# Three grouped attentions, from a loop of separate stages per group to one unrolled pipeline over all groups

## The chip, the cores and the metric

One core of one Trainium2 chip runs the whole program in one launch. The metric is the time of that launch on the device, in microseconds (us). TensorE (PE) multiplies, VectorE (DVE), ScalarE (ACT) and GpSimd (POOL) work on the results, SyncE (SP) issues the loads. Each engine runs its own instructions in their order in the program and waits only on semaphores.

## The reference

Four layers, each an attention and a feed-forward part, act on x (2 batches x 256 tokens x 512). Three attentions are dense and large; they are the ones that change:

```
x = x + attn0(norm(x), ctx)   # 32 heads of 128, 8 kv heads, rope, 512 keys
x = x + ffn0(norm(x))
x = x + attn1(norm(x), ctx)   # 16 heads of 96, 4 kv heads, keys = ctx + own (768)
x = x + ffn1(norm(x))
x = x + attn2(norm(x), ctx)   # 32 heads of 128, 4 kv heads, keys = ctx + own (768)
...
# one head: softmax(q @ k.T * scale + mask) @ v, then the heads' outputs @ wo
```

Two more layers' parts (ffn2, a small fourth attention, an 8-bit ffn3) follow.

## The kernel before

Every product is made from two planes of each operand, hi (rounded by ACT or POOL) and lo (what is left, by DVE or POOL), in three passes: hi by hi, lo by hi, hi by lo (`passes`, L299 to L301). The stages are called L0, L1 and L2 here. A stage runs over groups of four query heads: 8 groups in L0, 4 in L1, 8 in L2 (where two groups share one pair of key and value heads, `kv_every` 2). `Attention.loop` runs the groups in a hardware loop, the last one written out behind it.

Inside a group PE does, in this order: the four q projections, the k and v projections (each of 12 matmuls of 512 columns), then 16 score tiles in a pipeline of `PIPE` steps, and the four output projections `project(t)`. A score tile is 128 queries by 512 keys (L0) or 768 keys (L1, L2), and two tiles make one unit (one head and one batch). For tile i, step i holds `scores(i)`, `turn(i-2)` (the probabilities are transposed in pieces of four and two blocks, L563) and, at even i, `attend` of the unit whose tiles are i-4 and i-3 (L299 to L301 into `ps_o`).

DVE takes the largest score of each row (`nmax`, L754; in L0 one operation, L749, adds the mask, writes the tile to `l_p` and gives the largest), ACT takes the exponential (L681), DVE inverts its sum (L735), and the tile is scaled by ACT when even (L659), by DVE when odd (L759). After the transposes ACT makes the hi plane `l_pt_hi` (L669) and DVE the lo plane `l_pt_lo` (L777). In step i both engines do this for tile i-2, so that the planes of tile i-3 are done one step ahead of the `attend` that wants them. The transposes have three banks, `ps_t[p % 3]`.

L0 rotates its q and k: ACT swaps halves (L628, two operations), DVE multiplies with cos and sin (L707, L708), POOL adds (L477), ACT makes hi (L640) and DVE lo (L389, L387). The swap of the next tile is put ahead of the hi of this one. POOL also splits the loaded weights into their planes (L323, L325).

Of the kernel before, what the change touches and what calls it, by code (L numbers as in the profile page):

```python
# [20 lines left out]
ALU = mybir.AluOpType  # L21
# [7 lines left out]
P = 128  # L29
B, SQ, SK, D = 2, 256, 512, 512  # L30
T = B * SQ
# [35 lines left out]
def program(nc, A, out):  # L67
    ctx = ExitStack()
    with ctx:
# [44 lines left out]
        def attention_space(l):  # L114
# [9 lines left out]
            s.q = [take("q_hi", [P, HG, T], F32R), take("q_lo", [P, HG, T], F32R)]  # L124
# [3 lines left out]
            s.ot = [take("ot_hi", [P, HG, T], F32R), take("ot_lo", [P, HG, T], F32R)]  # L128
# [86 lines left out]
        ps_s = [ctx.enter_context(nc.psum_tensor(f"ps_s{i}", [P, 2, 512], F32)) for i in range(2)]  # L215
# [3 lines left out]
        ring = [ps_s[0][:, 0, :], ps_s[0][:, 1, :], ps_s[1][:, 0, :], ps_s[1][:, 1, :]]  # L219
# [30 lines left out]
        s_go = sem("tile_taken")  # L250
        s_rot = sem("rotation_parts")
        s_swap = sem("halves_swapped")
        s_nat = [sem("even_rows_in"), sem("odd_rows_in")]
# [3 lines left out]
        class Start:  # L257
# [3 lines left out]
            def __init__(self, g, hi, tile, piece, unit, q, kv, o, ra):  # L261
                self.g, self.hi, self.tile, self.piece, self.unit = g, hi, tile, piece, unit
                self.q, self.kv, self.o, self.ra = q, kv, o, ra
        counts = {n: 0 for n in ("g", "hi", "tile", "piece", "unit", "q", "kv", "o", "ra")}
# [8 lines left out]
        def attention_counts(l):  # L273
            n = l.groups
            kv = n // l.kv_every
            phase(l.name, g=kv * l.kv_tiles + n * 8, hi=kv * l.kv_hi + n * HG, tile=n * TILES,
                  piece=n * TILES * len(l.pieces), unit=n * UNITS, q=n, kv=kv, o=n,
                  ra=n * (HG + 2) if l.rope else 0)
# [121 lines left out]

        class Attention:
            def __init__(self, l, A, first_before, free=None):

                self.free = free
                self.l, self.s, self.c = l, SP[l.name], START[l.name]
                self.wkv, self.wq, self.wo = A[l.name + "_wkv"], A[l.name + "_wq"], A[l.name + "_wo"]
                self.first_before = first_before
                self.per = l.kv_every

            def loop(self, e, body):  # L410

                n = self.l.groups // self.per
                with e.Fori(0, n - 1) as i:
                    body(e, i, False)
                body(e, n - 1, True)

            def q_start(self, it, s):


                return it * (self.l.kv_tiles + 8 * self.per) + (self.c.g + (self.l.kv_tiles + 8 * s if s else 0))  # L420

            def o_start(self, it, s):
                return it * (self.l.kv_tiles + 8 * self.per) + (self.c.g + self.l.kv_tiles + 8 * s + HG)

            def hi_start(self, it, s):
                return it * (self.l.kv_hi + HG * self.per) + (self.c.hi + (self.l.kv_hi + HG * s if s else 0))

            def grp(self, it, s):
                return it * self.per + s
# [7 lines left out]
            def sp(self, e):  # L437
                l, c = self.l, self.c

                def body(e, it, last):  # L440
                    for s in range(self.per):
                        g = self.grp(it, s)
                        load(e, "o", None, self.wo[g], ("q", g + (c.q + 1)), parts=l.hd)
                        if s == self.per - 1 and not last:
                            load(e, "kv", None, self.wkv[it + 1], ("kv", it + (c.kv + 1)), cols=2 * l.hd)
                        if not (last and s == self.per - 1):
                            load(e, "q", None, self.wq[g + 1], ("o", g + (c.o + 1)), cols=HG * l.hd)
                self.loop(e, body)
# [12 lines left out]
            def pool(self, e):  # L461
                l, c, sp = self.l, self.c, self.s

                def body(e, it, last):
                    for s in range(self.per):
                        g = self.grp(it, s)
                        q0, o0 = self.q_start(it, s), self.o_start(it, s)
                        more = [("o", g + c.o, q0, p, l.hd, 512) for p in range(4)]
                        if s == self.per - 1 and not last:
                            more += [("kv", it + (c.kv + 1), o0, p, P, 2 * l.hd) for p in range(4)]  # L470
                        if not (last and s == self.per - 1):
                            more += [("q", g + (c.q + 1), o0, p, P, HG * l.hd) for p in range(4)]
                        if l.rope:
                            ra0 = it * (HG + 2) + c.ra
                            for t in range(HG + B):
                                e.wait_ge(s_rot, ra0 * 2 + (2 * t + 2))
                                e.tensor_tensor(sp.ra[:, t % 2, :], sp.ra[:, t % 2, :], sp.rb[:, t % 2, :], ALU.add)\  # L477
                                    .then_inc(s_ra, 1)
                        for job in more:
                            split(e, *job)  # L480
                self.loop(e, body)


            def pe(self, e):
# [3 lines left out]
                def body(e, it, last):  # L488
                    def bank(n, q0):

                        e.wait_ge(g_free, q0 + (n - 3))
                        return ring[n % 4]
                    for s in range(self.per):
                        g = self.grp(it, s)
                        q0, o0 = self.q_start(it, s), self.o_start(it, s)

                        def project_in(o, role, c0, src, lo, first=False):

                            for d in range(DK):
                                if first:  # L500
                                    e.wait_ge(g_free, c.g - 3 + d)
                                    e.wait_ge(w_rdy["q"], g * 8 + (8 * c.q + 2 * d + 2))
                                mm = passes(e, o[0:hd, :], planes(W[role], slice(None), d, slice(c0, c0 + hd)),
                                            planes(src, slice(None), d, slice(lo, lo + 512)), d == 0, d == DK - 1)
                            mm.then_inc(g_full, 1)
                        for hh in range(HG if s == 0 else HG - 1):
                            project_in(bank(hh, q0), "q", hh * hd, xT, 0, hh == 0)
                        if s == 0:

                            e.wait_ge(w_rdy["kv"], it * 8 + (8 * c.kv + 8))  # L510
                            e.wait_ge(s_csplit, DK)
                            for n, (src, lo) in enumerate([(cT, b * SK) for b in range(B)] + ([(xT, 0)] if l.self_keys else []), HG):
                                project_in(bank(n, q0), "kv", 0, src, lo)
# [1327 lines left out]
```

## Time and profile before

| | us |
|---|---|
| median of 3 runs | 2329.51 (2327.69 to 2330.35) |
| span of the profiled execution | 2328.4 |
| stage L0, first q projection to last output projection | 593.8 |
| stage L1 | 357.3 |
| stage L2 | 643.8 |
| one group of L0 after the first | 72.3 |
| one unit (two tiles) in the middle of an L2 group | 5.65 |

The stages' borders are the starts of their first projection matmul (18.7, 683.1 and 1084.3 us) and the ends of their last ones. The rest of the span, 733.5 us, is norms, feed-forward parts and the fourth attention. PE's busy time counts the modelled length of a matmul, which overlaps its neighbours' and can hide a short wait; the distance of two starts is the better measure of what one costs.

### The profile page before, as it was taken

Reading aid. Unit: us, or ns where it says so; the run is one execution under the profiler, and the core shown is the slowest. Engines: PE = TensorE matmul, PEld = TensorE weight load, DVE = VectorE, ACT = ScalarE, POOL = GpSimd, SP = SyncE. Lnnn points to the kernel's source line nnn. Section 1 sums busy time; section 2 is a strip of 40 time slices with the busy share of each in tenths; the row PEclk is TensorE's granted clock in tenths of the full one; section 3 lists DMA queues with packets and bytes.
Section 4 is the critical chain, followed back from the end, with each engine's and each line's share of the span. In section 5 each row is a group of like instructions: output and inputs, shape, how many; then the busy total and the mean of one; then the engine's idle time right before and its main releaser. Section 6 shows DMA issues by size and latency. Waiting matters only on the chain. (4 is left out here: it accounts for less than half of the span.)

```text
span 2328.4 us, 34351 instructions
## 1 busy us (share of the span) xinstructions
PE 2063.1 (89%) x11612; PEld 1707.9 (73%) x11616; DVE 1558.6 (67%) x3108; ACT 1142.4 (49%) x2338; POOL 901.6 (39%) x850
## 2 busy tenths in 40 slices
PE   5989999899879999987999999999988899996667
PEld 4777777777658788786888888888876677775535
DVE  5677666776657466475764674576564695897999
ACT  3556455565316256351653563555540594782430
POOL 7355533554432322224141233222316674662612
PEclk9999999999989999998999999999999999998889
DMA  3111001110110001001010011001101101002301
GB/s 137 46 45 45 18 27 45 45 36 18 62 30 25 14 22 34 19 12 62 28 37 20 28 37 32 33 19 39 37 28 43 37 1 55 1 19 77 127 18 37
DMA packets 20011, 87.16 MB, mean 37 GB/s; under 512 B 2736, under 2 KB 8624, under 8 KB 11440
## 3 DMA queue, kind: packets, MB, share of 16 engines
q1 hardware_dynamic: 19888, 85.55, 10.6%
q8 instruction: 74, 1.21, 0.2%
q14 instruction: 49, 0.40, 0.1%
HBM read 84.49 MB, written 1.05 MB: 37 GB/s over the span
## 5 line engine op out<-in xcount | busy, mean ns | idle before, releaser
L777 DVE TENSOR_TENSOR l_pt_lo<-ps_t,l_pt_hi 128x512 fp32r<-128x512 f32 (+1 forms) x512 | 283.2, 584 | 87.3 <-ACT l_pt_hi L669 80.1
L323 POOL TENSOR_TENSOR wo_hi<-raw_big,one 128x512 fp32r<-128x512 f32 (+2 forms) x116 | 123.0, 1060 | 489.6 <-PE ps_s L301 460.0
L669 ACT ACTIVATE l_pt_hi<-ps_t 128x512 fp32r<-128x512 f32 (+1 forms) x512 | 243.8, 515 | 108.1 <-PE ps_t L563 103.8
L563 PE MATMUL ps_t<-ident,l_p 128*128 128x128 f32 x1664 | 244.8, 277 | 45.9 <-DVE l_pt_lo L777 29.4
L563 PEld LDWEIGHTS ps_t<-ident,l_p 128*128 128x128 f32 x1664 | 191.9, 141 | 84.3 <-DVE l_pt_lo L777 37.7
L299 PE MATMUL ps_o<-l_pt_hi,l_v_hi 128*128 128x256 f32 (+1 forms) x704 | 211.7, 301 | 14.3 <-DVE l_pt_lo L777 14.3
L323 POOL TENSOR_TENSOR wq_hi<-raw_big,one 128x512 fp32r<-128x512 f32 (+1 forms) x120 | 126.1, 1051 | 199.7 <-PE ps_o L529 98.2
L299 PE MATMUL ps_s<-l_k_hi,l_q_hi 128*128 128x512 f32 (+3 forms) x512 | 195.9, 383 | 7.7 <-DVE l_k_lo L387 3.9
L754 DVE TENSOR_REDUCE nmax<-ps_s 128x1 f32<-128x768 f32 x192 | 183.0, 953 | 28.6 <-PE ps_s L301 28.3
L301 PE MATMUL ps_o<-l_pt_hi,l_v_lo 128*128 128x256 f32 (+1 forms) x704 | 200.0, 284 | 0.0
L300 PE MATMUL ps_o<-l_pt_lo,l_v_hi 128*128 128x256 f32 (+1 forms) x704 | 199.9, 284 | 0.0
L681 ACT ACTIVATE l_p<-ps_s,nmax 128x768 f32<-128x768 f32 x192 | 173.6, 904 | 28.2 <-DVE nmax L754 28.2
L477 POOL TENSOR_TENSOR l_ra<-l_ra,l_rb 128x512 f32<-128x512 f32 x48 | 76.3, 1591 | 271.8 <-DVE l_rb L708 270.7
L300 PE MATMUL ps_s<-l_k_lo,l_q_hi 128*128 128x512 f32 (+3 forms) x512 | 180.8, 353 | 0.0
L301 PE MATMUL ps_s<-l_k_hi,l_q_lo 128*128 128x512 f32 (+3 forms) x512 | 180.6, 353 | 0.0
L1125 POOL TENSOR_TENSOR l_p<-l_p,rinv 128x512 f32<-128x512 f32 x128 | 132.3, 1040 | 84.1 <-DVE rinv L1295 84.1
L299 PE MATMUL ps_s<-xT_hi,wq_hi 128*128 128x512 f32 (+1 forms) x384 | 152.6, 397 | 10.5 <-issue 10.0
L325 POOL TENSOR_TENSOR wq_lo<-raw_big,wq_hi 128x512 fp32r<-128x512 f32 (+1 forms) x120 | 156.4, 1303 | 9.4
L325 POOL TENSOR_TENSOR wo_lo<-raw_big,wo_hi 128x512 fp32r<-128x512 f32 (+2 forms) x116 | 152.0, 1310 | 9.1
L659 ACT ACTIVATE l_p<-l_p,rinv 128x768 f32<-128x768 f32 (+1 forms) x160 | 135.9, 849 | 34.9 <-DVE rinv L735 34.5
L299 PEld LDWEIGHTS ps_o<-l_pt_hi,l_v_hi 128*128 128x128 f32 (+1 forms) x704 | 130.2, 185 | 29.4 <-DVE l_pt_lo L777 21.2
L300 PE MATMUL ps_s<-xT_lo,wq_hi 128*128 128x512 f32 (+1 forms) x384 | 151.1, 394 | 0.0
(309 smaller groups left out, 5552.1 us busy)
## 6 DMA issues: line engine op xcount, KB each, us to landing
raw_big<-in_l_wq SPq DMA_DIRECT2D x18, 1024.0 KB, 5.0
raw_big<-in_l_wo SPq DMA_DIRECT2D x18, 1024.0 KB, 4.9
raw_big<-in_f_w SPq DMA_DIRECT2D x10, 1024.0 KB, 5.0
raw_kv<-in_l_wkv SPq DMA_DIRECT2D x12, 512.0 KB, 5.7
q_nat<-in_f_w1n SPq DMA_DIRECT2D x4, 1024.0 KB, 4.8
q_nat<-in_f_w2n SPq DMA_DIRECT2D x4, 1024.0 KB, 4.8
raw_big<-in_l_wq SPq DMA_DIRECT2D x4, 768.0 KB, 4.7
raw_big<-in_l_wo SPq DMA_DIRECT2D x4, 768.0 KB, 5.5
```

What stands on the lines that cost most here:

```text
L299: pe.matmul(o, a[0], b[0], start=start, stop=False)
L300: pe.matmul(o, a[0], b[1], start=False, stop=False)
L301: return pe.matmul(o, a[1], b[0], start=False, stop=stop)
L323: pool.tensor_tensor(hi, w, one[0:parts, 0:1].to_broadcast([parts, cols]), ALU.mult).then_inc(w_rdy[role], 1)
L325: pool.tensor_tensor(lo, w, hi.bitcast(F32), ALU.subtract).then_inc(w_rdy[role], 1)
L563: mm = e.transpose(ps_t[p % 3][:, k * P:(k + 1) * P], sp.p[:, i % 3, (k0 + k) * P:(k0 + k + 1) * P], ident[:, :])
L659: e.activation(pr, pr, ACT.Copy, scale=rinv[:, i - 1:i]).then_inc(s_scl[0], 1)
L669: e.activation(sp.pt[u % 2][0][:, k0:k0 + nk, qt * P:(qt + 1) * P], ps_t[p % 3][:, 0:nk * P].rearrange("p (k q) -> p k q", q=P), ACT.Copy) ...
L681: e.activation(sp.p[:, i % 3, :], src, ACT.Exp, bias=nmax[:, i:i + 1], scale=-1.0 if l.rope else 1.0, accum_out=rsum[:, i:i + 1]).then_inc ...
L754: e.tensor_reduce(nmax[:, i:i + 1], ps_flat(i)[:, 0:l.keys], AX.X, ALU.max, negate=True).then_inc(s_max, 1)
L777: e.tensor_tensor(pt[1], ps_t[p % 3][:, 0:nk * P].rearrange("p (k q) -> p k q", q=P), pt[0].bitcast(F32), ALU.subtract).then_inc(s_tlo, 1)
L1125: e.tensor_tensor(l3p[:, i % 4, :], l3p[:, i % 4, :], rinv[:, i % TILES:i % TILES + 1].to_broadcast([P, SK]), ALU.mult).then_inc(s3["scl"], 1)
```

## The change

The loops go. `Attention.place` writes one list of slots for all groups of a stage, one slot for each score tile (128 in L0, 64 in L1, 128 in L2), with a few before the first and four behind the last. The projections become jobs; each is cut into four parts of three matmuls, and the parts are dealt out over the slots of a neighbouring group: three parts a slot in L0 and L2, four in L1. In group g's slots run the output projections of group g-1, the q projections of group g+1, the key and value projections of batch 1 for this group and of batch 0 for the next. The jobs take turns on two banks, `ring[3]` and `ps_t[2]`, so the transposes have two banks in place of three. The own keys' projection of L1 and L2 (one of 512 columns) becomes two of 256.

The order within slot k is, with the engines' waits in brackets:

```
PE   scores(k) [largest or exp of k-2; the own keys' part also exp of k-1]
     job parts [job's bank]; values turned [bank]; turn(k-2) [bank: lo of the piece two before]
     even k: attend of tiles k-4, k-3 [lo of k-3]
ACT  hi of tile k-3; hi of the unit's output; L0: hi of the job ended in k-1 [POOL's add]
     exp(k); hi of values; job ended in k: swap or hi; even k: scale
DVE  largest(k) [scores(k)]; lo of tile k-3; lo of output; L0: lo of the job ended in k-1
     1/sum [exp(k)]; lo of values [their hi]; job ended in k: rotate [swap], lo, or add to x
     odd k: scale
POOL L0: add of the job ended in k; then pieces of weights
```

The core of the diff (of the two loops over the slots the first is PE's, the second DVE's):

```diff
-            s.q = [take("q_hi", [P, HG, T], F32R), take("q_lo", [P, HG, T], F32R)]
+            s.q = [[take(f"q{i}_{n}", [P, HG, T], F32R) for n in ("hi", "lo")] for i in range(2)]
-            s.ot = [take("ot_hi", [P, HG, T], F32R), take("ot_lo", [P, HG, T], F32R)]
-        ps_s = [ctx.enter_context(nc.psum_tensor(f"ps_s{i}", [P, 2, 512], F32)) for i in range(2)]
+        ps_s = ctx.enter_context(nc.psum_tensor("ps_s", [P, 4, 512], F32))
+        ORDER = {
+            "l0": ["k1 o0 o1 v1 o2 o3 q0 k0 q1 v0 q2 q3"],
+            "l1": ["k1 K1 o0 v1 V1 o1 o2 o3 q0 k0 K0 q1 v0 V0 q2 q3"],
+            "l2": ["k1 K1 o0 v1 V1 o1 o2 o3 q0 q1 q2 q3", "o0 o1 o2 o3 q0 q1 k0 K0 q2 v0 V0 q3"],
+        }
+        FIRST = {"l0": "q0 q1 q2 q3 k0 v0", "l1": "q0 k0 K0 q1 v0 V0 q2 q3", "l2": "q0 k0 K0 q1 v0 V0 q2 q3"}
...
+                            job(name, own, [g * TILES + (4 * n + part) // per for part in range(4)])
...
+            def bank(self, j):
+                return (ring[3], ps_t[2][:, :])[j.n % 2]
...
+                def take_turn_bank(p):
+                    if p >= 2:
+                        e.wait_ge(s_tlo, c.piece + p - 1)
+                    return ps_t[p % 2]
...
+                for k in self.slots:
+                    if 0 <= k < self.N:
+                        scores(k)
+                    for j, part in self.parts.get(k, ()):
+                        project(j, part)
+                    for j in self.values.get(k, ()):
+                        turn_values(j)
+                    if 0 <= k - 2 < self.N:
+                        turn(k - 2)
+                    if self.unit_at(k) is not None:
+                        attend(self.unit_at(k))
...
+                for k in self.slots:
+                    if 0 <= k < self.N:
+                        largest(k)
+                    if 0 <= k - 3 < self.N:
+                        turned_lo(k - 3)
...
+                    for j in self.ended.get(k - 1, ()):
+                        if j.rope is not None:
+                            operand_lo(j, sp.ra[:, j.rope % 2, :], s_qk)
...
+                    for j in self.values.get(k, ()):
+                        e.wait_ge(s_thi, c.piece + self.v_piece[j.n] + 1)
...
+                    for j in self.ended.get(k, ()):
+                        if j.rope is not None:
+                            rotate(j)
```

The outputs of a group are written over its own q planes, and q has two sets of planes. In the job names a capital letter is an own-key job of 256 columns. The fourth attention uses the same banks under other names.

## Rows read from the trace of the kernel before

**Rows 1.** The page: the span.
```profile
span 2328.4 us, 34351 instructions
```

**Rows 2.** The stretches view: start:end, length, busy of PE, PEld, DVE, ACT, POOL, clock, DMA.
```profile
18.70:612.50 593.80, 538.53 (x2882) 439.80 (x2881) 393.55 (x853) 329.95 (x678) 282.75 (x245) 0.98 0.10 35
683.10:1040.40 357.30, 343.97 (x2066) 288.60 (x2064) 208.69 (x400) 176.38 (x362) 87.01 (x96) 0.99 0.08 23
1084.30:1728.10 643.80, 619.85 (x3794) 546.51 (x3792) 396.20 (x745) 338.83 (x698) 167.53 (x160) 1.00 0.09 30
104.00:176.30 72.30, 66.45 (x361) 54.39 (x360) 48.14 (x106) 40.67 (x84) 33.98 (x30) 1.00 0.10 36
...
176.33:187.21 10.88, 10.88 (x50) 9.01 (x48) 5.15 (x9) 4.82 (x8) 2.96 (x2) 1.00 0.00 0
...
227.36:231.61 4.25, 3.96 (x29) 3.38 (x28) 3.75 (x11) 3.58 (x9) 0.00 (x0) 1.00 0.18 75
1460.02:1465.67 5.65, 5.65 (x44) 5.34 (x43) 4.99 (x12) 4.77 (x10) 0.00 (x0) 1.00 0.01 3
```

**Rows 3.** The timeline of PE in an L2 unit: start, length, then the instruction.
```profile
1460.02 0.40 PE L299 MATMUL ps_s<-l_k_hi,l_q_hi 128*128 128x512 f32 x1
...
1461.07 0.82 PE L563 MATMUL ps_t<-ident,l_p 128*128 128x128 f32 x6
1461.64 0.47 PE L299 MATMUL ps_s<-l_k_hi,l_q_hi 128*128 128x512 f32 x1
...
1462.77 0.82 PE L563 MATMUL ps_t<-ident,l_p 128*128 128x128 f32 x6
1463.41 0.38 PE L299 MATMUL ps_o<-l_pt_hi,l_v_hi 128*128 128x256 f32 x1
```

**Rows 4.** The waits of PE in stage L0: us in total, times, longest.
```profile
PE ps_o L299 <- DVE l_pt_lo L777: 14.3, 29, 0.8
PE ps_t L563 <- DVE l_v_lo L387: 9.7, 8, 1.3
```

**Rows 5.** The waits of PE in stage L2.
```profile
PE ps_t L563 <- DVE l_pt_lo L777: 20.0, 23, 1.7
```

**Rows 6.** The timeline of PE where one L0 group ends and the next begins.
```profile
176.10 0.39 PE L301 MATMUL ps_s<-wo_hi,l_ot_lo 128*128 128x512 f32 x1
176.33 0.39 PE L299 MATMUL ps_s<-xT_hi,wq_hi 128*128 128x512 f32 x1
```

**Rows 7.** The timeline of DVE in the same L2 unit.
```profile
1461.27 0.96 DVE L754 TENSOR_REDUCE nmax<-ps_s 128x1 f32<-128x768 f32 x1 [0.21 <-PE ps_s L301]
1462.34 1.02 DVE L777 TENSOR_TENSOR l_pt_lo<-ps_t,l_pt_hi 128x512 fp32r<-128x512 f32 x2
```

**Rows 8.** The timeline of DVE in an L0 unit.
```profile
228.44 0.69 DVE L749 CUSTOM_DVE_ANT_0 l_p<-ps_s,l_mask 128x512 f32<-128x512 f32 x1
...
229.32 0.69 DVE L777 TENSOR_TENSOR l_pt_lo<-ps_t,l_pt_hi 128x512 fp32r<-128x512 f32 x1 [0.18 <-ACT l_pt_hi L669]
```

**Rows 9.** The timeline of all engines in the start of stage L0.
```profile
36.45 2.48 POOL L477 TENSOR_TENSOR l_ra<-l_ra,l_rb 128x512 f32<-128x512 f32 x2
...
37.74 0.63 ACT L640 ACTIVATE l_q_hi<-l_ra 128x512 fp32r<-128x512 f32 x1 [11.86 <-POOL l_ra L477]
38.40 1.21 ACT L628 ACTIVATE l_rb<-ps_s 64x512 f32<-64x512 f32 x2
...
40.25 0.68 DVE L708 TENSOR_TENSOR l_rb<-l_rb,l_sin 128x512 f32<-128x512 f32 x1
...
41.01 1.66 POOL L477 TENSOR_TENSOR l_ra<-l_ra,l_rb 128x512 f32<-128x512 f32 x1 [2.07 <-DVE l_rb L708]
...
52.59 0.50 PE L299 MATMUL ps_s<-l_k_hi,l_q_hi 128*128 128x512 f32 x1 [0.48 <-DVE l_k_lo L387]
```

**Rows 10.** The timeline of ACT in the same L2 unit.
```profile
1462.46 0.91 ACT L681 ACTIVATE l_p<-ps_s,nmax 128x768 f32<-128x768 f32 x1
1463.25 0.21 ACT L681 ACTIVATION_READ_ACCUMULATOR l_p<-ps_s,nmax 128x1 f32 x1
```

More of the change, by code:

```diff
@@ L438, in sp @@
                 l, c = self.l, self.c
[L440 to L448, printed above, removed]
+                for g in range(l.groups):
+                    before = self.raw_before(g)
+                    if g + 1 < l.groups:
+                        load(e, "q", None, self.wq[g + 1], before, cols=HG * l.hd)
+                        before = ("q", c.q + g + 2)
+                    kv = g // l.kv_every
+                    if g % l.kv_every == 0 and kv + 1 < self.kvs:
+                        load(e, "kv", None, self.wkv[kv + 1], ("kv", c.kv + kv + 1), cols=2 * l.hd)
+                    load(e, "o", None, self.wo[g], before, parts=l.hd)
             def pool_first(self, e):
@@ L462, in pool @@
                 l, c, sp = self.l, self.c, self.s
[L464 to L480, printed above, removed]
@@ new lines, in own_o @@
+                def own_o(g, piece):
+                    used = self.full(self.find["o", g - 1, 3, False]) if g else c.g
+                    split(e, "o", c.o + g, used, piece, parts=l.hd)
+                if not l.rope:
+                    for g in range(l.groups):
+                        for piece in range(4):
+                            next_q(g, piece)
+                        for piece in range(4):
+                            next_kv(g, piece)
+                        for piece in range(4):
+                            own_o(g, piece)
+                    return
@@ new lines, in project_out @@
+                def project_out(j):
+                    e.wait_ge(g_full, self.full(j))
+                    if j.kind == "v":
+                        if j.stage >= 4:
+                            old = [v for v in self.jobs if v.stage == j.stage - 4][0]
+                            e.wait_ge(s_T, c.piece + self.v_piece[old.n] + 1)
+                        e.tensor_copy(xn[0:hd, j.stage % 4, 0:j.width], self.bank(j)[0:hd, 0:j.width]).then_inc(g_free, 1)
+                        return
+                    t = j.i
+                    if j.g:
+                        e.wait_ge(g_free, self.full(self.find["o", j.g - 1, t, False]))
+                    e.tensor_tensor(x[:, t, :], self.bank(j), x[:, t, :], ALU.add).then_inc(g_free, 1)
+                    if j.g == l.groups - 1 and t < TT - 1:
+                        e.wait_ge(g_free, self.full(j))
+                        e.bn_stats(st[:, t, :], x[:, t, :])
```

631 lines of the change are left out of this document (317 added, 314 removed).

## The prediction

> **What bounds the kernel now.** I read the stretches view first. The three attention stages fill 593.8 + 357.3 + 643.8 = 1594.9 us of the 2328.4 us span [rows 1, 2]; the other 733.5 us are code that the change leaves alone. In them PE is busy 91%, 96% and 96%, while DVE has 66%, 58% and 62% and ACT and POOL less: PE sets the pace, and what a rewrite can win is only the time in which PE waits. Next I priced PE's work by distances between starts. Four q projections, 48 matmuls, take 10.88 us [rows 2]: one job 2.72, one part of three matmuls 0.68. An L2 unit takes 5.65, of which about 0.07 is a wait (the second turn lasts 1462.77 to 1463.41, 0.64, the first 0.57) [rows 2, 3]: 5.58. For an L0 unit I scale the pieces of that one (12 products 1.5, six score matmuls 1.44, two turns 0.76): 3.7 of the 4.25 measured [rows 2].
>
> Work per group is then: L0 8 x 3.7 + 12 x 2.72 + 0.8 (values turned) = 63.0; L1 8 x 5.58 + 14 x 2.72 + 1 = 83.7; two groups of L2 16 x 5.58 + 22 x 2.72 + 1 = 150.1. Stages: 504, 335 and 600, 1439 together. PE stands still for the rest: 90, 22 and 44 us, 156 in all. That is the most the change could win. The waits views name the owners: in L0 products that wait for DVE's lo planes (14.3) and transposes behind the values (9.7) [rows 4], in L2 transposes that wait for lo planes, 20.0 [rows 5]. A unit inside a group waits little; most of the loss lies where a group fills and drains.
>
> **What the change removes.** Filling and draining happen once a stage. The branch at the end of a group is removed too, and by the rows it costs nothing: the first matmul of a new group starts 0.23 us after the last of the old, the normal distance [rows 6]. The Trainium skill ("Runtime: NRT & Kernel Launch", Instruction fetch mechanics) says that a taken branch outside the window forces a fetch, so that unrolling helps; by that rule the 13 branches would each give something back, by the row they give 0. I put in 0.
>
> The number of matmuls stays, but for the own-key jobs (24 of 512 columns become 48 of 256): +0.5 us a stage. The loads are the same in number and size. SP issues the next q's before this group's o's; POOL is busy 34 of 72.3 us in an L0 group [rows 2], and each weight is split at least two slots ahead of its first use, so I cost that order at nothing.
>
> **What it adds: a chain inside each slot of L1 and L2.** With two turn banks and two pieces a tile, the first piece of turn(k-2) needs the lo of tile k-3's first piece. DVE makes that in slot k, behind largest(k), which waits for this slot's scores. From the rows: DVE starts its largest 1.25 after the scores began [rows 3, 7], takes 0.96, then the lo 0.69 [rows 7, 8]: 2.90 after the slot's start, about 2.85 since neighbours on DVE overlap a little. PE's scores end at 1.05 (1460.02 to 1461.07) or, behind a turn, 1.13 (1461.64 to 1462.77) [rows 3]. With three full parts PE gets to the turn at 3.1: hidden, by 0.2. With m parts it waits 1.8 - 0.68 m. The same chain stood one step earlier before, since both engines did tile i-2 in step i. So a slot without jobs costs nearly what a full one does, and the work that lies in the prologue (8 jobs) and the tail (4 jobs) is missing in the slots without making them shorter. L1: 12 empty slots x 1.8 = 21.6. L2: in the first group 0.4 + 1.8 + 0.4 + 5.4 + 1.1, in the last 1.1 + 10 x 1.8: 28.3. Jobs of half width leave gaps too: 7 x 0.4 = 2.8 in L1, 2.6 for each of four key and value pairs in L2, 10.
>
> **Values in the turn ring.** A slot that turns values puts their piece between two of the probabilities', so the second piece of turn(k-2) needs DVE's lo of the values. The values are turned at about 3.3, plus 0.2 to ACT, 0.63 hi, 0.69 lo [rows 8, 9]: 4.8 against 3.7 for PE, and the gap before them besides; 1.6 lost for a full job, 0.7 for the half one behind it. Seven such pairs in each of L1 and L2: 16 each.
>
> **L0's rope chain.** One piece a tile frees the turn bank a slot earlier, but ACT now makes hi of the last rotated job before exp(k), and exp(k) stands before the next swap; before, the swap went ahead. Rotations in neighbouring slots follow each other by: POOL's add 1.24 (two in 2.48) to 1.66, taken 1.5; hi 0.63; exp 0.83 (the 768-wide one is 0.91 [rows 10]); swap 1.21; two multiplications 1.3; handovers 0.1: 5.5 [rows 9]. A slot of PE is 3.1 (odd) or 4.65 (even). Jobs end in slots 9, 10, 11. The first is rotated 5.0 after slot 9 began, the third 11.0 later, the scale adds 0.6: 16.6, where PE's three slots take 10.9. DVE comes 5.7 late to slot 12, then does largest and lo (1.4) [rows 8], and attend, which PE would reach at 3.2, starts 3.9 late. The pair in 14 and 15, held up by the values' lo in 14, costs 2.7, the one in 17 0.7: 7.4 for each of seven groups, 52, and 1 in the last. The old loss was 9.3 (72.3 - 63.0). Empty pairs of slots take 6.2 here (DVE's chain through exp and scale), not 3.7: six of them, 15. In the start the adds begin at 36.45 as before [rows 9]; then each rotation waits for hi of the one before: 4.75 each. The first scores come at 58.0, not 52.6 [rows 9]: 39.3 us for six jobs of 2.72, so 23 of wait.
>
> **Changes of operand.** Scores behind a turn cost 0.08 more than behind products [rows 3]; inside projections there is nothing. New seams, one or two a slot: between 0 and 0.08, taken 0.05, x 320 slots = 16 (6, 3, 6). Tails 3, 2, 3; L2's start at the lower clock 3, as now.
>
> **The sum.** L0: 504 + 23 + 53 + 15 + 3 + 6 = 604, against 593.8: +10. L1: 335 + 0.5 + 21.6 + 2.8 + 16 + 2 + 3 = 381, against 357.3: +24. L2: 600 + 0.5 + 28.3 + 10 + 16 + 3 + 3 + 6 = 667, against 643.8: +23. Together +57 on the profiled 2328.4: 2385; the median of the runs is 1.1 higher, so 2387.
>
> **Rivals.**
> *DVE late in full slots too.* The cover there is 0.2 us, and odd slots end with an operand's lo and the scale. If DVE starts 0.4 later than that cover in each of the 96 even slots of L1 and L2, that is +38: 2425. For it: POOL's splits run beside DVE's operations. Against it: in the steady unit of L2 DVE is busy 4.99 of 5.65 and still on time [rows 2], and the new full pair is 9.7 long.
> *The rope chain stays hidden.* If PE never sees it (it would, once the period is over 3.9), L0 loses 53 less: 2334. Against it: the 5.5 is a sum of measured pieces.
> *A full pipeline.* The other sign: the lo chain is not what ends PE's wait in a slot, so that PE runs at its work. It decides from there: if lo of tile k-3 is done by the end of the scores, as it is now, a slot costs its matmuls. Then 1439 + start 23 + tails 8 + seams 16 = 1486, 109 less than now: 2220. For it: DVE and ACT have a third of their time free. Against it: the order of DVE's slot puts largest first, and that can't start before the scores.
>
> **How the numbers follow.** A difference under 0.2% (4.7 us) can't be told from none here. Forecast 0.65; late DVE 0.15; hidden rope 0.12; full pipeline 0.08. The bounds of single terms: seams 0 to 26 for 16, rope 45 to 60, the values' 32 down to 20, empty slots 45 to 70: 2350 to 2410 for the forecast alone. With most of the late-DVE case and without hidden rope and full pipeline, the range is 2345 to 2430. Faster: 0.08 and a little of the rope case, 0.10; same: the rest of the rope case, 0.08; slower 0.82.
>
> **What would show it.** In the last group of L2 two neighbouring slots should take about 9.2 us with no job in them (5.65 now), PE waiting for `l_pt_lo` before the first transposes. Full pairs should take 9.7 to 9.8. The slot with values should show a wait of more than 1 us in the middle of a turn, for `l_v_lo`. In L0 the products of slot 12 should start some 3 us late behind lo planes, with DVE idle for the swap before. The first scores of L0 should come near 58. I am wrong if empty slots are shorter than 4 us on average, or if PE's waits for lo planes shrink in L2.

## The result, and the profile after

The changed kernel takes 2410.7 us (median; 2409.4 to 2415.7) beside 2329.4 us before: a ratio of 1.0353, 95% interval 1.0339 to 1.0368. The forecast was 2387 in a range of 2345 to 2430. The sign and the mechanism were right; 22 us of waits and of lower clock were missing from the sum, which named 57 us where the profiled executions show 79 (2407.6 against 2328.4); on the medians it is 24 us short.

The page's span, and the stretches view of the three stages, which answers to [rows 1, 2] (from the first q projection to the last matmul of the last output projection):

```profile
span 2407.6 us, 32169 instructions
...
19.88:631.85 611.97, 544.94 (x2880) 460.11 (x2880) 379.67 (x850) 335.35 (x676) 272.05 (x244) 0.94 0.10 34
701.39:1084.22 382.83, 350.80 (x2162) 296.03 (x2160) 208.40 (x403) 179.96 (x370) 87.84 (x96) 0.98 0.07 21
1130.61:1808.68 678.07, 623.64 (x3890) 545.01 (x3888) 387.80 (x755) 344.90 (x706) 169.83 (x160) 0.99 0.08 29
```

Before, the same stages ran 18.74 to 612.74, 683.13 to 1038.18 and 1084.28 to 1727.65. The end of L1 in [rows 2], 1040.40, and with it the 357.3 of the table of the time before, is 2.2 too late: the stage before was 355.1 us long, and the sum's +24 for L1 is +26 against that. So L0 ends 19.1 later (1.1 of it at its start), L1 is 27.8 longer, L2 34.7, and the stretches between and behind them are 2.4 shorter: 79.2. TensorE's share fell from 91, 97 and 96% to 89, 92 and 92%.

The stretches view of single slots and groups says where. In order: one L0 group; a pair of L2 slots without a job; a full pair; the L2 slot in which values are turned; slot 12 of the L0 group, and the products at its end; slot 8 of L2's first group:

```profile
122.09:194.03 71.94, 67.23 (x364) 57.39 (x362) 47.58 (x106) 41.45 (x85) 32.87 (x30) 0.95 0.11 37
...
1749.24:1758.67 9.43, 5.95 (x44) 5.33 (x43) 4.96 (x10) 4.93 (x10) 6.93 (x13) 1.00 0.28 112
1250.46:1260.14 9.68, 9.68 (x63) 8.58 (x62) 5.32 (x12) 4.94 (x10) 1.54 (x2) 1.00 0.00 1
...
1298.50:1305.94 7.44, 6.22 (x46) 5.39 (x45) 4.18 (x8) 4.10 (x8) 0.00 (x0) 1.00 0.01 2
...
173.52:182.39 8.87, 6.15 (x31) 5.37 (x29) 5.39 (x12) 5.67 (x11) 4.78 (x5) 0.84 0.00 1
179.69:182.39 2.70, 2.70 (x12) 2.70 (x13) 0.92 (x2) 2.39 (x5) 2.62 (x3) 0.50 0.00 0
...
1186.92:1196.08 9.16, 7.42 (x32) 6.86 (x31) 2.89 (x5) 3.07 (x6) 5.26 (x5) 0.50 0.30 102
```

A pair without any projection costs 9.43 us, a pair with six parts in it (one and a half jobs, 18 matmuls) 9.68: the slot is as long as a chain, not as long as its matmuls. The waits view of PE in the stage L0, then in L2, answers to [rows 4, 5]:

```profile
PE ps_o L298 <- DVE l_pt_lo L801: 41.4, 20, 2.8
PE ps_t L298 <- DVE l_ra L826: 11.5, 2, 10.9
...
PE ps_t L687 <- DVE l_pt_lo L801: 34.8, 38, 1.8
PE ps_t L687 <- DVE l_v_lo L863: 10.1, 14, 1.0
PE ps_t L694 <- DVE l_pt_lo L801: 4.0, 8, 1.6
PE ps_s L298 <- DVE l_q_lo L853: 3.7, 4, 0.9
```

In L0 the products' wait for lo planes went from 14.3 to 41.4 us, in L2 that of the transposes from 20.0 to 34.8. (The 10.9 for `l_ra` stands in the start of L0, at 40.5 us, where a key projection waits for a bank that a rotation has to free.) How an empty slot of L2 runs, in the timeline of PE and then of DVE (the bracket holds the idle time before the instruction and its releaser); compare [rows 3, 7]:

```profile
1758.67 0.40 PE L298 MATMUL ps_s<-l_k_hi,l_q_hi 128*128 128x512 f32 x1
...
1759.61 0.28 PE L300 MATMUL ps_s<-l_k_hi,l_q_lo 128*128 128x256 f32 x1
1761.62 0.85 PE L687 MATMUL ps_t<-ident,l_p 128*128 128x128 f32 x6 [1.74 <-DVE l_pt_lo L801]
1762.23 0.48 PE L298 MATMUL ps_s<-l_k_hi,l_q_hi 128*128 128x512 f32 x1
```
```profile
1759.92 0.96 DVE L793 TENSOR_REDUCE nmax<-ps_s 128x1 f32<-128x768 f32 x1 [3.60 <-PE ps_s L300]
1760.80 1.01 DVE L801 TENSOR_TENSOR l_pt_lo<-ps_t,l_pt_hi 128x512 fp32r<-128x512 f32 x2
```

DVE sits idle for 3.60 us until this slot's scores are done, takes their largest, and only then the lo planes of a tile that ScalarE had ready long before; PE has nothing left to do and waits 1.74 us for them. The sum had 1.8.

### The profile page after: what moved, and what is told of

It is laid out like the page before. It is cut to its first block and busy times, and to the rows that moved or that the text cites. A ratio compares the mean times of both kernels' runs of the same rounds, so it can differ in the third digit from the quotient of the medians.

```text
span 2407.6 us, 32169 instructions
## 1 busy us (share of the span) xinstructions
PE 2074.9 (86%) x11804; PEld 1730.7 (72%) x11808; DVE 1546.4 (64%) x3132; ACT 1158.5 (48%) x2354; POOL 894.6 (37%) x850
## 5 line engine op out<-in xcount | busy, mean ns | idle before, releaser
L687 PE MATMUL ps_t<-ident,l_p 128*128 128x128 f32 x1664 | 245.0, 277 | 79.6 <-DVE l_pt_lo L801 59.9
L298 PE MATMUL ps_o<-l_pt_hi,l_v_hi 128*128 128x256 f32 (+1 forms) x832 | 254.7, 306 | 42.3 <-DVE l_pt_lo L801 41.4
L300 PE MATMUL ps_o<-l_pt_hi,l_v_lo 128*128 128x256 f32 (+1 forms) x832 | 242.1, 291 | 0.0
L299 PE MATMUL ps_o<-l_pt_lo,l_v_hi 128*128 128x256 f32 (+1 forms) x832 | 241.8, 291 | 0.0
L298 PEld LDWEIGHTS ps_o<-l_pt_hi,l_v_hi 128*128 128x128 f32 (+1 forms) x832 | 159.2, 191 | 49.5 <-DVE l_pt_lo L801 49.2
L589 POOL TENSOR_TENSOR l_ra<-l_ra,l_rb 128x512 f32<-128x512 f32 x48 | 66.5, 1385 | 254.7 <-DVE l_ra L826 254.7
L300 PEld LDWEIGHTS ps_o<-l_pt_hi,l_v_lo 128*128 128x128 f32 (+1 forms) x832 | 160.7, 193 | 0.0
L299 PEld LDWEIGHTS ps_o<-l_pt_lo,l_v_hi 128*128 128x128 f32 (+1 forms) x832 | 160.4, 193 | 0.1
```

What stands on the lines that cost most here:

```text
L298: pe.matmul(o, a[0], b[0], start=start, stop=False)
L299: pe.matmul(o, a[0], b[1], start=False, stop=False)
L300: return pe.matmul(o, a[1], b[0], start=False, stop=stop)
L687: mm = e.transpose(o[:, kk * P:(kk + 1) * P], sp.p[:, k % 3, at:at + P], ident[:, :])
```

## The experiments

All times are medians of runs, against 2328 to 2330 for the kernel before in the same session. Stage lengths are from the stretches view, in us (L1 and L2 as above; L0 from its first q projection):

| kernel | L0 | L1 | L2 | time | ratio to before |
|---|---|---|---|---|---|
| before | 594.0 | 355.1 | 643.4 | 2329.4 | |
| changed | 612.0 | 382.8 | 678.1 | 2410.7 | 1.0353 |
| 1 lower parts first | 605.8 | 373.9 | 669.9 | 2388.9 | 1.0254 [1.0236, 1.0271] |
| 5 scaling deferred | 591.9 | 366.7 | 643.0 | 2340.6 | 1.0042 [1.0025, 1.0059] |
| 6 values early | 584.4 | 355.4 | 629.4 | 2305.8 | 0.9900 [0.9882, 0.9918] |
| 7 upper part late | 581.1 | 355.5 | 629.5 | 2303.0 | 0.9893 [0.9875, 0.9910] |
| 10 swap early | 551.6 | 355.8 | 629.6 | 2274.5 | 0.9763 [0.9750, 0.9776] |

**1. Lower parts first.** VectorE takes the lo of tile k-3 before the largest of tile k:

```diff
                 for k in self.slots:
-                    if 0 <= k < self.N:
-                        largest(k)
                     if 0 <= k - 3 < self.N:
                         turned_lo(k - 3)
+                    if 0 <= k < self.N:
+                        largest(k)
```

> Only DVE's order in a slot changes: the lo planes of tile k-3 come ahead of largest(k), in all three stages. Theory 1 (the lo chain behind the scores): a pair of empty slots in L2, 9.43 us now, falls to about 7.8 (the scale of the odd tile then holds the next lo), full pairs stay at 9.69, the slots with values lose at most 0.3; L1 falls by about 15 us, L2 by about 20, L0 by about 19 because every product after a cluster of rotations starts 0.7 earlier; in all about 2358. Rival (PE is held by job banks or by late weights, not by the lo planes): empty pairs stay at 9.4 and the time within 5 us of 2411. Rival (PE's own work and seams are the bound): no change either.

Measured: 2388.9, 22 us less than the changed kernel. The chain was real, since its order alone moved every stage, but the gain was smaller than expected: an empty pair of L2 still took 9.1 us on average (7.64, 1.63, 6.19, 2.36, 7.85, 1.62 for six neighbouring slots of the last group). The timeline of DVE there, and one row of ACT's, show the next holder; the last row is PE's in a slot with values:

```profile
1732.51 0.94 DVE L793 TENSOR_REDUCE nmax<-ps_s 128x1 f32<-128x768 f32 x1
1734.51 0.17 DVE L860 RECIPROCAL rinv<-rsum 128x1 f32<-128x1 f32 x1 [1.06 <-ACT l_p L753]
1736.16 1.02 DVE L801 TENSOR_TENSOR l_pt_lo<-ps_t,l_pt_hi 128x512 fp32r<-128x512 f32 x2 [1.49 <-ACT l_pt_hi L735]
...
1734.71 0.94 ACT L775 ACTIVATE l_p<-l_p,rinv 128x768 f32<-128x768 f32 x1 [0.23 <-DVE rinv L860]
...
1282.36 0.44 PE L687 MATMUL ps_t<-ident,l_p 128*128 128x128 f32 x2 [2.08 <-DVE l_v_lo L863]
```

Largest, exp, reciprocal and scale of one tile stand in one slot, each on the other engine than the one before; the hi and then the lo of an older tile are queued behind them. The slots with values got longer too: the seven of L2 took 8.1 to 9.6 in place of 7.44, some 12 us in all where 0.3 a slot had been allowed for. The largest now came later, with it the exp, and behind the exp the hi and lo of the values: PE waited 2.08 for them in the slot of the row, where it had waited 0.97, and 19.8 us in all of L2 in place of 10.1.

**2. The swap first.** In L0 the swapped copy is made before the hi of the job before it, and the rotation before its lo:

```diff
-  ACT: hi of job ended in k-1; exp(k); ...; swap of job ended in k; scale
+  ACT: exp(k); ...; swap of job ended in k; hi of job ended in k-1; scale
-  DVE: lo of job ended in k-1; 1/sum(k); ...; rotate; scale
+  DVE: 1/sum(k); ...; rotate; lo of job ended in k-1; scale
```

> Only L0 changes: ACT swaps the job ended in slot k ahead of the hi of the job before it, and DVE rotates ahead of that job's lo, as in the kernel before. Theory 2 (the chain add, hi, exp, swap, rotate sets L0's stalls): the first scores come about 4.5 us earlier, near 52.5; the distance of two rotations in neighbouring slots falls only from 5.5 to about 5.1, since largest, exp, swap, rotate, lo and scale still follow one another, so L0 falls by 10 to 15 us in all. Rival (POOL's add is the whole stall): the slots after 9, 10 and 11 lose their 4 us, L0 falls by 30 or more. L1 and L2 stay within 1 us.

Measured: 2414.4 in a single run. The first scores came 5.4 us earlier (51.60 against 57.04) and L0 ended 4.6 earlier, its inner groups as long as before (71.8 in the mean, both times). The gain in the start is shown; in the groups the order of these two changed nothing. That the whole is not shorter lies in parts that the edit doesn't touch: L1 was 4.7 longer, since one of its first slots fell to the lower clock and took 9.16 in place of 6.74, and the one two behind it 8.21 in place of 6.65; the stretches outside the three stages were 5 longer; L2 was the same. A difference of 4 us in one run is not worth reading further.

**3. The rotation a slot later**, on top of experiment 1: a job that ends in slot k is rotated at the head of slot k+1 and split in k+2; k0 is projected second.

```diff
+  DVE: lo(k-3); rotate job ended in k-1; largest(k); lo of job ended in k-2; ...
+        FIRST = {"l0": "q0 k0 q1 q2 q3 v0", ...
```

> On top of lo first: in L0 a job ended in slot k is swapped in slot k, rotated by DVE in slot k+1 ahead of largest, and split in slot k+2; the first key job moves up to second place in the prologue so that the first scores don't wait for its lo. Theory 2: the rope chain no longer stands inside one slot, its stalls of 7 us a group shrink to about 1, the first scores come near 51; L0 falls by about 50 us below that of lo first, the whole to about 2310. Rival (L0 is held by DVE's total work or by the job banks): L0 stays within 10 us of that of lo first.

Measured: 2417.0, ratio 1.0376 [1.0359, 1.0394]. Wrong by 107 us, with the sign wrong. The first scores came at 51.24, but each inner group of L0 took 75.1 us. The waits view of PE in L0, a row of its timeline, and the stretch behind that row:

```profile
PE ps_s L298 <- DVE l_ra L828: 38.7, 21, 3.8
...
207.84 0.50 PE L298 MATMUL ps_s<-wo_hi,l_q_hi 128*128 128x512 f32 x1 [3.75 <-DVE l_ra L828]
...
209.00:212.00 3.00, 3.00 (x17) 2.90 (x15) 1.46 (x3) 1.68 (x5) 2.92 (x4) 0.53 0.00 0
```

The rotation also frees the job's bank, and there are only two of them: moved by a slot, it holds up the projections. (The place of k0 was changed in the same run; it bears on the first scores, not on the inner groups.) What I had weighed was only who waits for the rotated operand.

**4. L2 without most of its q projections**, in the changed kernel. This kernel leaves out 11 of the 12 matmuls of each q projection of L2's groups 2 to 7 (264 matmuls, at 0.227 each 59.9 us of TensorE's work), so its output differs.

```diff
+                        if l is L2 and j.g >= 2:
+                            if part == 3:
+                                e.matmul(o[0:hd, :], W["q"][0][:, part, ...], xT[0][:, part, 0:T], ...).then_inc(g_full, 1)
+                            return
```

> Leaves out part of the computation: in L2 the q projections of groups 2 to 7 do one matmul of twelve, so 264 matmuls of 512 columns are gone, 59.9 us of PE's work at 0.227 each; jobs, banks and waits stay. Theory 1: the slots that held these parts become empty slots, which cost nearly as much as full ones (9.43 against 9.69 a pair), so L2 falls by only 4 to 8 us. Rival (PE's work is the bound in full slots and the chain has slack): L2 falls by 40 to 60 us.

Measured: 2407.3 in a single run, 3.4 us less for 59.9 us of work, and not even these in L2: that stage took 677.9 where it had 678.1, and L0, which the edit doesn't touch, was 2.4 shorter. Emptied pairs of slots took 5.87 + 3.56 = 9.43, and PE's waits for lo planes in L2 took over what the work had filled (34.8 us, 38 times, in the changed kernel):

```profile
PE ps_t L692 <- DVE l_pt_lo L806: 78.0, 66, 2.3
```

What the emptied pairs gave, 0.25 each, was lost again, in part in slot 12 of the third and fifth groups, which took 7.9 in place of 6.1 with a wait of 2.3 in it. So in the changed kernel this work of TensorE in L2 has no price of its own. This is the run that decides for the chain.

**5. Scaling deferred**, on top of 1: reciprocal and scale of tile k-1 stand in slot k.

```diff
   DVE: 
+       1/sum(k-1)
        lo(k-3); lo of the output; largest(k)
+       scale(k-1) if odd
-       1/sum(k) ... scale(k) if odd
   ACT: hi(k-3); hi of the output; hi of rotated job
+       scale(k-1) if even
        exp(k)
-       ... scale(k) if even
```

> The pipeline as changed, with the lower parts of the turned tile ahead of the largest on VectorE (as in the first experiment), and with the reciprocal of the row sums and the scaling of tile k-1 moved from the end of slot k-1 into slot k, so that no engine waits inside a slot for scores, largest, exp, reciprocal and scale in a row. Theory 1 (slots are as long as the in-order chain of their engines, and the first experiment only gave the chain another holder, the largest, exp, reciprocal and scale of an odd tile): an empty pair of L2 falls from 9.2 to between 5.7 and 7 us, L1 to about 360 us, L2 to about 645, the full pairs of L2 stay at 9.69; in all 2330 to 2350. Rival (TensorE is held by its clock or by turn banks whatever the order): empty pairs stay at 9 us, in all 2385 or more.

Measured: 2340.6, 48 us less than 1. An empty pair of L2 now takes 5.80 + 1.62 = 7.42 (expected 5.7 to 7, a little short of the truth), a full one still 9.68, the stage 643.0 as expected; L1 took 366.7 where 360 had been expected. Of the 27 us that L2 lost against 1, about 12 lie in the seven slots with values, which take 7.3 again (8.5 in the first group).

**6. Values early**, on top of 5: they are turned behind the scores, and their hi and lo are not kept behind exp and the projections' end.

```diff
   PE:  scores(k)
+       turn_values
        project parts
-       turn_values
   ACT: 
+       hi of values
        exp(k)
-       hi of values
   DVE: largest(k)
+       lo of values
        scale(k-1) if odd; ...
-       lo of values
```

> The kernel of the run with deferred scaling, and the values of a slot are turned on TensorE right after the scores, their upper part taken on ScalarE ahead of the exp and their lower part on VectorE right behind the largest. Theory 1: the slots with values in them (4 a group in L1, 2 a group of keys in L2) lose the wait of TensorE for the lower part of the values, about 1.8 us each, so some 14 us in L1 and 14 in L2 and little in L0: in all 20 to 30 us less than the run before it. Rival (the wait passes to the turn bank of the tile behind it): less than 8 us.

Measured: 2305.8, 35 us less than 5, and 1.0% less than the kernel before. L1 lost 11.3, L2 13.5, L0 7.5; the pair with the values in it went from 7.32 + 4.64 to 6.18 + 3.93 in L2. More than expected by L0's part, for which I had put in little.

**7. The upper part late**, on top of 6: in L0 ScalarE takes the hi of the rotated operand behind exp(k) in place of ahead of it, so that exp doesn't wait for GpSimd's addition.

```diff
-  ACT: hi of job ended in k-1; ...; exp(k); swap
+  ACT: ...; exp(k); hi of job ended in k-1; swap
```

> The kernel of the run with early values, and the upper part of a rotated operand of L0 is taken on ScalarE behind the exp in place of ahead of it, so that the exp of a slot doesn't wait for GpSimd's addition. L1 and L2 have no such step and stay as they are. Theory 1 (the long slots of L0, 7.5 to 8.9 us against 4.7 in the others, come from the rotation's chain ending ahead of the exp): slots 0 and 12 of each group fall to 5 to 6 us, L0 20 to 30 us shorter than in the run before it. Rival (the chain is only late elsewhere: its lower part then ends the slot, or scores wait for the operand): L0 changes by less than 5 us.

Measured: 2303.0; L0 3.3 us shorter. The rival was right: slot 12 went from 7.6 to 7.1, slot 14 from 5.2 to 5.9. Even the 3.3 are no gain of the new order inside the groups: in kernel 6 four of the six inner groups took 68.1 and two, with a longer slot 12, took 69.6 and 70.9; in kernel 7 all six took 68.4 to 68.5. The timeline of DVE in front of slot 12's products, then of PE, shows the waits that were left:

```profile
306.75 0.69 DVE L809 TENSOR_TENSOR l_k_lo<-l_ra,l_k_hi 128x512 fp32r<-128x512 f32 x1 [1.41 <-ACT l_k_hi L762]
307.99 0.69 DVE L825 TENSOR_TENSOR l_rb<-l_rb,l_sin 128x512 f32<-128x512 f32 x1 [0.54 <-ACT l_rb L771]
...
310.04 0.35 PE L298 MATMUL ps_o<-l_pt_hi,l_v_hi 128*128 128x256 f32 x1 [2.15 <-DVE l_pt_lo L802]
```

**8. Experiment 4's omission again, in kernel 7** (the same 264 matmuls left out, the diff is that of 4).

> The kernel of the run with the late upper part, in which the q projections of L2's groups 2 to 7 do one of their twelve matmuls: the same 264 matmuls, 59.9 us of TensorE's work, that were left out of the changed kernel for a gain of 3.4 us. Theory 1 (after the reordering TensorE itself sets the length of L2's full slots, 9.69 us a pair, and the chain of a slot without projections is 5.8 us a pair): nearly the whole of the work comes back as time, between 45 and 60 us less, about 2250. Rival (the slots are still bound by a chain of the other engines): less than 15 us.

Measured: 2280.0, 23 us less where the changed kernel gave 3.4 (L2 by itself 26 less, where the changed kernel gave 0.2). Between the two theories. In the full slots of kernel 7 TensorE is busy 75.67 of 76.00 us (the stretch 1200 to 1276 of its trace, the first row below), so there it is the bound; once the work is out, the next chains are met soon: an emptied pair took between 7.0 and 9.7 (5.10 + 1.86 in the second group, 7.78 + 1.87 in the fifth), and slot 8 of the second group, behind an emptied one, 7.19 in place of 6.02. In the stretch 1150 to 1600 PE waited 9.6 us for ScalarE's exp and 9.3 for lo planes (second and third row), where in kernel 7 it had waited 1.0 in all. Of the 59.9 us TensorE bound 23; the rest was already covered by chains just below it.

```profile
1200.00:1276.00 76.00, 75.67 (x502) 68.28 (x501) 50.54 (x101) 43.14 (x91) 14.86 (x16) 1.00 0.08 32
...
PE ps_s L298 <- ACT l_p L761: 9.6, 15, 0.9
PE ps_t L692 <- DVE l_pt_lo L807: 9.3, 12, 1.3
```

**9. The key second**, on top of 7.

```diff
-        FIRST = {"l0": "q0 q1 q2 q3 k0 v0", ...
+        FIRST = {"l0": "q0 k0 q1 q2 q3 v0", ...
```

> The kernel of the run with the late upper part, with one order changed: the six first projections of L0 run as q0, k0, q1, q2, q3, v0 in place of q0 to q3, k0, v0. The first scores need q0 and k0, and waited 4.4 us for k0's lower part. Theory 1 (the chain of k0's rotation holds the first scores): first scores 3 to 4.4 us earlier and 2299 in all. Rival (the first six projections wait for one another's banks whatever their order, or k0's weights come later than q's): no change, 2303.

Measured: 2306.4, ratio 0.9905 [0.9891, 0.9918]: no difference from 7 that can be told. The first scores came 1.8 earlier (55.36), and the first group of L0 took 66.2 in place of 61.1, 3.0 of it in its slot 0. Here earlier first scores were worth nothing, since the first slots were longer by more.

**10. The swap early**, on top of 7: swap and rotation of the job that ends in slot k stand ahead of exp(k).

```diff
   ACT: hi of values
+       swap of job ended in k
        exp(k); hi of job ended in k-1
-       swap of job ended in k
   DVE: largest(k); lo of values; scale(k-1) if odd
+       rotate job ended in k          [also waits until ra's last reader is done]
        lo of job ended in k-1
-       rotate job ended in k
```

> The kernel of the run with the late upper part (2303), and in L0 the swapped copy of a projection that ends in slot k is made on ScalarE ahead of the exp of slot k, with VectorE's rotation right behind the largest and the lower part of the operand before it after that; L1 and L2 stay as they are. In the slots with a rotation VectorE there waited 1.0 to 1.4 us for the upper part and 0.54 for the swap, and a chain of three such slots ended with TensorE waiting 2.1 us for the turned tile (slot 12 of each L0 group, 7.1 us against 4.7). Theory 1 (these two waits inside the slot make the period of a rotation 5.5 us): slot 12 falls to 5 us and slots 0 and 2 to 4.7, L0 15 to 30 us shorter, in all 2273 to 2288. Rival (ScalarE, with swap, exp and upper parts in a row, takes VectorE's place, or GpSimd's addition is what is late): less than 5 us either way.

Measured: 2274.5, 28 us less than 7 and 2.4% less than before. L0 is 29.5 shorter than in 7. Inner L0 groups take 65.1 us (72.3 before, 71.9 after the change, 68.4 in 7), slot 12 5.4, slot 2 4.7, slot 0 5.4 where 4.7 had been expected; about 10 of the 29.5 lie in the start and the first group (first scores 51.4 against 57.2, the group 56.8 against 61.1). The stretches view of its stages, and the waits of PE in L0 from 105 to 540:

```profile
19.89:571.45 551.56, 521.80 (x2880) 440.63 (x2880) 389.36 (x850) 329.33 (x676) 283.16 (x244) 0.99 0.11 38
643.86:999.65 355.79, 343.42 (x2162) 292.89 (x2160) 208.42 (x404) 177.75 (x370) 87.72 (x96) 0.99 0.08 23
1046.17:1675.78 629.61, 613.84 (x3890) 544.42 (x3888) 392.55 (x756) 341.17 (x706) 169.79 (x160) 1.00 0.08 31
...
PE ps_o L298 <- DVE l_pt_lo L803: 7.7, 15, 1.7
```

**11. The splits after the scale**, in the changed kernel: GpSimd begins the next q weights of L1 and L2 after VectorE's last scale of the group.

```diff
                     for g in range(l.groups):
+                        if g:
+                            e.wait_ge(s_scl[1], (c.tile + TILES * g) // 2)
```

> The changed kernel with one wait more: in L1 and L2 GpSimd begins the splits of a group's next q weights after VectorE has scaled the last tile of the group before. In the changed kernel this scale (TENSOR_SCALAR, 768 columns) took 1.70 us where it stood beside GpSimd's splits and 0.61 elsewhere, and TensorE then waited 0.78 us for the turned tile in slot 0 of L2's odd groups (7.0 us against 6.0). Theory 1 (the two engines get in each other's way, and this is what the four slots lose): the scale takes 0.61 in those four places, slot 0 of the odd groups 6.0, L2 4 us shorter, in all 2407. Rival (slot 0 is long because four q projections ended before it, whatever GpSimd does): the slots stay at 7.0 and the total at 2411.

Measured: 2412.4, ratio 1.0361 [1.0342, 1.0380], and L2 675.7 against 678.1. Below, DVE's scale and GpSimd's split in the changed kernel and PE's wait behind them; then the same scale in this one.

```profile
1229.72 1.70 DVE L876 TENSOR_SCALAR l_p<-l_p,rinv 128x768 f32<-128x768 f32 x1
...
1229.72 1.29 POOL L324 TENSOR_TENSOR wq_lo<-raw_big,wq_hi 128x512 fp32r<-128x512 f32 x1
...
1233.03 0.85 PE L687 MATMUL ps_t<-ident,l_p 128*128 128x128 f32 x6 [0.78 <-DVE l_pt_lo L801]
```
```profile
1232.46 0.61 DVE L878 TENSOR_SCALAR l_p<-l_p,rinv 128x768 f32<-128x768 f32 x1
```

The mechanism is shown: the scale takes 0.61, slot 0 of the second, fourth and sixth groups 6.03, 6.00 and 6.01 in place of 7.0. They are three, not four: the last group has no next weights, and its slot 0 took 6.03 in the changed kernel too. L2 is 2.4 shorter, three times 1.0 less three times 0.2 in slot 2. In the total this can't be seen: L0, which the edit doesn't touch, was 614.7 in this profile against 612.0.

## Why the prediction was right in sign and 22 us short

**PE sets the pace, and only its waits can be won.** Right for the kernel before. For the changed one it holds no longer: experiment 4 took 59.9 us of PE's work out of L2 and left its length as it was.

**The chain in each slot of L1 and L2.** Right, and the decisive step. Forecast: 1.8 of wait in an empty slot, 9.2 a pair, full pairs 9.7 to 9.8; measured 1.74, 9.43 and 9.68. The pair is 0.23 over the forecast because PE's own work in it is 5.95 and not the 5.58 that I took from a unit nearly without a wait; the two waits are 0.12 shorter. L1 came to 382.8 where the sum had 381. No run gave the transposes their third bank back, so what two banks cost by themselves, beside the order of the engines, stays open.

**Values in the turn ring.** Right: PE's wait for `l_v_lo` in the middle of a turn, 0.97 and then 0.50 (I had 1.6 and 0.7 with the gap before), the slot 7.44 in place of 6.0 and the one behind it 4.64 in place of 3.7. The claim of "more than 1 us" for one wait was a little high. Experiment 6 is its test. PE's two waits, in the slot with values and in the one behind it:

```profile
1303.51 0.44 PE L687 MATMUL ps_t<-ident,l_p 128*128 128x128 f32 x2 [0.97 <-DVE l_v_lo L863]
...
1310.37 0.44 PE L687 MATMUL ps_t<-ident,l_p 128*128 128x128 f32 x2 [0.50 <-DVE l_v_lo L863]
```

**Full slots are covered.** Right for most and wrong in two places of each odd group of L2, and this was the first term that is missing, 8 us. In slot 0 of three of them the cover of 0.2 was gone, by GpSimd: 1.0 each (experiment 11). The rival "DVE late in full slots" had the right reason in three slots and not in 96. In slot 3 of all four PE waited 0.94 for the lo of the last unit's output, which o2's last part reads (`ps_s <- l_q_lo`, 3.7 in all): 4.90 against 3.69, 1.2 each. The sum had no term for where the o projections stand, and it took for granted that POOL's splits cost DVE nothing in a full slot.

**L2's start.** The sum had 3 us for the lower clock, as before. Slot 8 of the first group is an empty slot at a granted clock of 0.50 and took 9.16, not 5.87: 3.3 more. PE had been busy 1.95 of the 3.92 us before it. With the 8 of the odd groups this comes to the 11 us by which L2 passed its 667.

**L0's rope chain.** The mechanism is shown by experiment 10; 2 and 7 alone did little for the groups. The products of slot 12 started 2.72 late (the sum had 3.9, the claim "some 3"); slots 0 and 1 took 11.5 and slots 12 and 13 took 12.2, where a full pair is 7.8, and slots 6, 10 and 14 some 0.4 more than their neighbours: 71.9 a group, where the forecast came to 71.1 (63.0 of work, 7.4 and the seams). The lateness was 1.2 smaller than in the sum, and as much was paid in a way that the sum didn't know: in six of the seven groups TensorE came out of the wait at the lower clock, and the twelve products took up to 2.70 in place of 1.5 (the row 179.69 to 182.39). In front of them stood DVE's wait for the swap, as forecast:

```profile
176.69 0.69 DVE L824 TENSOR_TENSOR l_rb<-l_rb,l_sin 128x512 f32<-128x512 f32 x1 [1.07 <-ACT l_rb L766]
...
178.91 0.69 DVE L801 TENSOR_TENSOR l_pt_lo<-ps_t,l_pt_hi 128x512 fp32r<-128x512 f32 x1
...
179.69 0.55 PE L298 MATMUL ps_o<-l_pt_hi,l_v_hi 128*128 128x256 f32 x1 [2.72 <-DVE l_pt_lo L801]
```

L0 passed its 604 by 8: the start 2 better than forecast (first scores 57.04 against 58.0, begun 1.1 later), six inner groups 4 worse, and the first group, the last and the tail 6 worse, the term that was sized worst in this stage.

**The seams and the slips.** The 16 us for seams can't be found in full pairs: one of L2 takes 9.69, where the unit and six parts come to 9.66, one of L0 7.80 against 7.78. In L0 the slots 6, 10 and 14 cost more than that term. Three additions of the prediction are off, none of them by enough to matter for the total: 3.9, 2.7 and 0.7 are 7.3 and not 7.4, L2's empty slots come to 28.2, and the lower bounds of the single terms taken together give 2331 and not 2350.

**The branch at the end of a group.** By the rows it was worth nothing, and what the stages lost is accounted for by slots without a gain to set against it. That is weaker than a test; none was made of it alone.

**The rivals.** That the rope chain stays hidden (0.12) is refuted by the products of slot 12. A full pipeline at 2220 was the far rival, with a chance of 0.08, and its condition was the right one to name: lo of tile k-3 done by the end of the scores. Experiment 1 fulfilled it by order and found the next chain; it took the edits of order 1, 5, 6, 7 and 10, none of them of work, to come to 2274.5. There the three stages take 551.6 + 355.8 + 629.6 = 1537.0, where the rival's sum had 1486. So the loss of 79 us was not the pipeline's but its order inside the slot: the same work in another order is 136 us shorter. Where the 136 came from can be read off the stretches: PE's idle time fell from 153.5 to 57.9, and its busy time from 1519.4 to 1479.1 for the same 8932 matmuls, 40 us, as its clock rose (0.94, 0.98 and 0.99 became 0.99, 0.99 and 1.00).

## What to carry to other kernels

In a software pipeline whose engines run in order, write down for every slot the longest path over engines that must be walked inside one slot, and give each step of it that can wait a slot of its own, with work that is ready ahead of work that is not; only then does the busiest engine's work count. Before you move a step, list every resource that its end frees as well as who reads its result: the bank was what made experiment 3 fail. To learn whether an engine bounds a stage, take a known amount of its work out; 0.2 us of the stage for 60 us of work said more than any share of busy time.

## What the hardware showed that was not expected

**A wait of TensorE can cost twice.** After 2.72 us of idle time the granted clock was 0.50 for the next 2.70 us: the lower of its two levels, 1.2 GHz, for work that came late already. After 3.75 us (experiment 3, at 207.84) it was 1.00 for 1.2 us and then 0.53 for 3 us. The length of the wait alone doesn't decide it. Of the seven waits of 2.72 to 2.76 us in the changed L0, the fourth was followed by a clock of 1.00, and its slot took 7.68 in place of 8.7 to 8.9; the waits of 1.74 us at the end of L2 kept 1.00, but ahead of slot 8 of its first group the clock fell to 0.50, and the longest wait in the 3.9 us before had been 1.65. What does decide it no run here isolates. The stretches behind the third and the fourth of the seven waits, the same products each time:

```profile
251.78:254.48 2.70, 2.70 (x13) 2.70 (x14) 0.93 (x2) 2.38 (x5) 2.62 (x3) 0.50 0.00 0
323.87:326.57 2.70, 2.70 (x18) 2.48 (x19) 1.22 (x3) 2.42 (x6) 2.62 (x3) 1.00 0.00 0
```

Between the changed kernel and that of experiment 10 the busy time of the same matmuls differs by 40 us, beside 96 of idle time.

**VectorE and GpSimd block each other on some operations.** VectorE's scale of 768 columns took 0.61 us alone and 1.70 where GpSimd's splits ran; in kernel 7 the lo of a q operand, both of whose inputs lie in SBUF, took 0.69 alone and 1.82 beside them:

```profile
369.68 0.69 DVE L811 SCALAR_TENSOR_TENSOR l_q_lo<-l_ra,l_q_hi 128x512 fp32r<-128x512 f32 x1 [1.00 <-ACT l_q_hi L762]
...
380.39 1.82 DVE L811 SCALAR_TENSOR_TENSOR l_q_lo<-l_ra,l_q_hi 128x512 fp32r<-128x512 f32 x1 [1.00 <-ACT l_q_hi L762]
...
380.37 1.29 POOL L324 TENSOR_TENSOR wo_lo<-raw_big,wo_hi 128x512 fp32r<-128x512 f32 x1
```

The largest (0.94 at 1231.35, 0.96 elsewhere) and the lo planes out of PSUM (1.01 both ways) kept their times beside the same splits. The Trainium skill ("SBUF — State Buffer", Who interferes with whom) says that a VectorE instruction in a two-port mode and a GpSimd instruction block each other for the whole instruction, whichever was issued first, and that one with two SBUF inputs contends with a GpSimd instruction that reads SBUF. The trace agrees with both, and adds a price. Where the two began together (1229.72, shown with experiment 11, and 380.39 here) VectorE lost 1.1 us beside a GpSimd operation of 1.29. In slot 0 of the third group of the changed kernel's L2 the scale began 0.5 us into one and lost 0.60:

```profile
1310.98 1.21 DVE L876 TENSOR_SCALAR l_p<-l_p,rinv 128x768 f32<-128x768 f32 x1
...
1310.48 1.29 POOL L324 TENSOR_TENSOR wq_lo<-raw_big,wq_hi 128x512 fp32r<-128x512 f32 x1
```

So what is lost here is about the rest of the GpSimd operation under way. What it means where VectorE has little cover: 1.1 us of VectorE was 1.0 of the slot where the cover was 0.2.
